# Message passing over 212,500 edges on one core: the main loop's transposes written as ordinary matmuls with the identity

## What is computed

```python
h = relu(layernorm(x))
def layer(h, row, col, dist, ...):
    edge_in = concatenate([h[row], h[col], dist], axis=1)      # 129 columns
    e = silu(edge_in @ eW1 + eb1)                              # 128 hidden
    e = silu(e @ eW2 + eb2)
    agg = segment_sum(e, row, num_segments=12500)
    node_in = concatenate([h, agg], axis=1)
    return silu(node_in @ nW1 + nb1) @ nW2 + nb2
out = x + layer(h, src, dst, edge_weight1, ...)
```

## Time and profile before

| | |
|---|---|
| median of 3 runs | 3044.79 us |
| the three runs | 3040.09, 3044.79, 11595.62 us |
| profiled execution, span from the first to the last instruction | 3042.3 us |
| PE busy | 2652.8 us (87%), 21703 matmuls |
| PEld busy | 2068.1 us (68%), 21704 weight loads |
| DVE busy | 2125.5 us (70%) |
| ACT busy | 1601.7 us (53%) |
| POOL busy | 2012.3 us (66%) |
| mean granted TensorE clock | 0.986 of full speed |

### The profile page before, as it was taken

The page is one execution under the profiler, slowest core; times in us unless marked ns, Lnnn a source line. Parts: engine busy times, 40 slices in busy tenths (PEclk is TensorE's granted clock), DMA queues, the critical chain, the costliest instruction groups (busy, mean ns, idle before and its releaser), DMA issues.

```text
span 3042.3 us, 77490 instructions
## 1 busy us (share of the span) xinstructions
PE 2652.8 (87%) x21703; PEld 2068.1 (68%) x21704; DVE 2125.5 (70%) x7337; ACT 1601.7 (53%) x3366; POOL 2012.3 (66%) x2075
## 2 busy tenths in 40 slices
PE   7899999999688888888888888888888888888899
PEld 4555555555477777777777777777777777777776
DVE  8999999997566666666666666666666666666665
ACT  3677777777344444444444444444444444444455
POOL 1254444445677777777777777777777777777772
PEclk7999999999799999999999999999999999999999
DMA  3011111111222222222222222222222222222343
GB/s 94 20 40 27 39 28 39 34 34 30 48 59 59 60 57 59 59 60 59 58 59 59 60 60 58 58 60 59 59 59 59 59 59 58 58 59 55 77 120 103
DMA packets 366054, 171.78 MB, mean 56 GB/s; under 512 B 289494, under 2 KB 330126, under 8 KB 365934
## 3 DMA queue, kind: packets, MB, share of 16 engines
q0 software_dynamic: 69600, 123.49, 15.4%
q1 hardware_dynamic: 274142, 36.29, 7.8%
q10 hardware_dynamic: 22192, 10.53, 1.2%
HBM read 139.11 MB, written 31.04 MB: 56 GB/s over the span
## 4 chain that ended last, share of the span: by engine, by line
PE 81%; issue 11%; ACT 4%; DVE 3%; DMA 1%; POOL 0%; ACTq 0%; SPq 0%; DVEq 0%; POOLq 0%
PE bk L1208 16%; PE bk L1228 15%; PE bk L1219 13%; PE bk L1206 9%; PE bk L1196 5%; PE bk L1071 4%; PE bk L1217 3%; PE bk L1105 3%; PE bk L1137 2%; PE bk L1059 2%; PE bk L1060 2%; PE bk L1239 1%; ACT BIG L1354 1%; PE bk L1099 1%; PE bk L1274 1%
## 5 line engine op out<-in xcount | busy, mean ns | idle before, releaser
L554 POOL DMA_INDIRECT GA<-q_d,IX x1758 | 1671.5, 951 | 545.4 <-issue 533.3
L920 DVE SCALAR_TENSOR_TENSOR GA<-c_bc,EW,GA 128x128 f32<-128x128 f32 x1758 | 558.5, 349 | 432.7 <-DMA GA<-q_d,IX 429.2
L929 DVE TENSOR_TENSOR BIG<-bk,BIG 128x128 f32 x1758 | 511.4, 291 | 345.1 <-issue 156.4
L1206 PE MATMUL bk<-identf,GA 128*128 128x128 f32 x1758 | 501.2, 285 | 253.8 <-issue 240.3
L1208 PE MATMUL bk<-OHS,P 128*128 128x128 bf16 x5274 | 695.8, 225 | 0.1
L1443 ACT ACTIVATE ED<-bk,eb1c 128x512 f32<-128x512 f32 x440 | 302.1, 687 | 703.0 <-PE bk L1208 698.7
L1208 PEld LDWEIGHTS bk<-OHS,P 128*128 x5274 | 501.3, 96 | 111.3 <-issue 0.2
L1228 PE MATMUL bk<-ED 128*128 128x128 f32 x3516 | 504.7, 287 | 0.0
L519 POOL DMA_INDIRECT rec_d<-BIG,GA x208 | 246.8, 1187 | 376.9 <-issue 285.6
L1219 PEld LDWEIGHTS bk<-W,ED 128*128 128x128 f32 x3516 | 464.8, 193 | 24.3 <-issue 7.6
L1206 PEld LDWEIGHTS bk<-identf,GA 128*128 128x128 f32 x1758 | 247.5, 141 | 321.7 <-issue 297.2
(11 more groups left out here) (247 smaller groups left out, 2761.9 us busy)
## 6 DMA issues: line engine op xcount, KB each, us to landing
GA<-q_d,IX POOLq DMA_INDIRECT x1758, 2.5
q_d<-QS SPq DMA_DIRECT2D x14, 448.0 KB, 3.1
u_d<-QS ACTq DMA_DIRECT2D x98, 64.0 KB
OHS<-u_d SPq DMA_DIRECT2D x18, 256.0 KB, 3.1
rec_d<-ED SPq DMA_DIRECT2D x16, 220.0 KB, 9.6
RW<-rec_d SPq DMA_DIRECT2D x110, 32.0 KB
rec_d<-BIG,GA POOLq DMA_INDIRECT x208, 2.4
HT<-hT_d ACTq DMA_DIRECT2D x99, 32.0 KB
```

The costliest lines, as they stand in the source:

```text
L554: e.indirect_dma_start(G[k % 4 * U + u], None, q_d, bass.IndirectOffsetOnAxis(ap=IX[g // BG % 2][:, k * U + u:k * U + u + 1], axis=0))\
L920: ins = e.scalar_tensor_tensor(out=G[k % 4 * U + u], in0=c_bc[:, :], scalar=ew[:, w:w + 1], in1=G[k % 4 * U + u], op0=ALU.mult, op1=ALU.add)
L929: e.tensor_tensor(AGG[:, ds(v, P)], banks[6 + k % 2][:, u * P:(u + 1) * P], AGG[:, ds(v, P)], ALU.add).then_inc(s["ad"], 1)
L1206: e.matmul(z, G[k * U + u], identf[:, :], is_transpose=True, start=True, stop=False)
```

## The change

The diff is complete. `TPb` becomes the whole of bank 0 as fp32, so that the turned one-hots stand there as fp32 values; `tcopy` is not touched and reads them as fp32. In `mA` the four bf16 transposes become ordinary bf16 matmuls with the identity, and in `mB` the fp32 transpose that opens each tile's sum becomes an ordinary fp32 matmul with the identity. The waits, the order and all other work stay.

```diff
@@ -263,7 +263,7 @@
-        TPb = banks[0][:, :].bitcast(bf16)[:, 0:512]
+        TPb = banks[0]
@@ -1193,7 +1193,7 @@
                 for u in range(tiles(g)):
-                    last = e.transpose(TPb[:, u * P:(u + 1) * P], OHb[k][:, u, :], identb[:, :])
+                    last = e.matmul(TPb[:, u * P:(u + 1) * P], OHb[k][:, u, :], identb[:, :], start=True, stop=True)
                 last.then_inc(s["tp"], 1)
@@ -1203,7 +1203,7 @@
                     z = banks[2][:, u * P:(u + 1) * P]
-                    e.matmul(z, G[k * U + u], identf[:, :], is_transpose=True, start=True, stop=False)
+                    e.matmul(z, G[k * U + u], identf[:, :], start=True, stop=False)
                     for q in range(3):
                         last = e.matmul(z, P3[q][:, ds(v, HF)], OHT[k % 2][:, u * P:(u + 1) * P],
                                         start=False, stop=(q == 2))
```

## The result

The changed kernel takes 3051.69 us (median of 8 runs, 3050.11 to 3053.89); the kernel before, run beside it, 3040.68 us (median of its 8; one of them, 11595.62 us, is far off and left out of the ratio; without it the median is 3040.12). The ratio is 1.0037, 95% interval [1.0028, 1.0046]: 11.0 us slower, or 0.37%, and within 2%. The interval reaches from 8.5 to 14.0 us. The forecast was +10.6 us. The 3055 us that were predicted start from 3044.79 us, a median of three runs, and lie 3.3 us too high; that starting point alone is 4 us too high. The profiled execution has a span of 3050.3 us and took 3052.16 us.

The account below looks back on a forecast made before the run. POOL's gathers were taken to bound the loop and PE the end: zero in the loop and for the one-hots, 9.8 plus 0.8 us at the end, together +10.6 us, predicted 3055 us, range 3046 to 3080.

Parts of the forecast that it names:

- What bounds the loop: In the main loop POOL's gathers, four of 1.25 us, set a group's time of 5.0 us, although PE looks busier.
- I am wrong if POOL waits for PE in the loop: Sign against the forecast in the main loop, where POOL was expected to have almost no wait for PE.
- Two instructions for one: In `mB` each fp32 transpose becomes an ordinary matmul of two instructions, so line 1206 shows 3516 instead of 1758.
- The price of a tile: Each `mB` tile gains 0.12 us of PE work (0.11 to 0.13), 0.48 us a group; wider bounds 0.06 to 0.24.
- The threshold for 2%: In the loop, roughly 0.18 us extra a tile would make the kernel slower by over 2% (61 us).
- The loop's slack: PE needs 19.75 us for four loop groups, POOL gives 20.1: 0.3 us to spare, no time added, idle 0.57 to 0.1.
- the two rivals that break it: In the loop PE overtakes POOL, about 3230 us, chance 0.09; or lands just over its pace, near 3075, chance 0.07.
- The end: In the last, unrolled groups PE sets the time: 20.5 groups add 9.8 us, three groups before them 0.8 us.
- The one-hots at zero: In `mA` ordinary bf16 matmuls cost the same as bf16 transposes, and ACT's copy from the fp32 bank adds zero.
- The rule of a fourfold transpose: Rival: `mB`'s ordinary fp32 matmul costs four times the transpose, 0.44 us against 0.11, giving 3389 us; chance 0.02.

Follow-up runs that it names:

- e3b: The changed kernel with the gathered rows of the last 24 groups back on fp32 transposes: 3040.92 us, ratio 0.9998 to the kernel before.
- e9: The changed kernel with one more ordinary fp32 matmul of the same rows ahead of each loop tile's own, result overwritten: 3081.87 us, ratio 1.0134 to the kernel before.
- the first comparison: Follow-up runs on a chip of their own, against the kernel before, with the changes tried by halves and by loop or end; the kernel before took 3562 us there.
- e6: The changed kernel with a group's four ordinary fp32 matmuls issued first and its twelve bf16 matmuls behind them: 3048.03 us, ratio 1.0023 to the kernel before.
- e4b: The changed kernel with fp32 transposes of gathered rows in the loop, ordinary fp32 matmuls in the last 24 groups alone: 3052.97 us, ratio 1.0038 to the kernel before.
- the second comparison: Follow-up runs on another chip, e3b, e4b and e6 among them, against the kernel before, which took 3041 us there.
- e7: The kernel before with a group's four fp32 transposes issued ahead of its twelve bf16 matmuls: 3039.86 us, ratio 0.9999 to the kernel before.
- e1: The changed kernel with fp32 transposes kept for the gathered rows, only the one-hots' transposes made ordinary matmuls: 3562.99 us, ratio 1.000 to the kernel before.

## Why the prediction was right, and where its steps were off

**What bounds the loop: right.** POOL's waits named it against the busy shares, e3b shows that the loop's ordinary matmuls are free, and e9 that the next step past the limit is paid. "I am wrong if POOL waits for PE in the loop" did come true on the chip of the first comparison, where the kernel before waits too.

**Two instructions for one: right,** 3516 of them.

**The price of a tile: right in kind, mis-sized.** The term was 0.12 us (0.11 to 0.13), from fp32 matmuls that stand in a row. Where it is paid, a tile went from 0.285 to 0.445 us, 0.16 more, but the group's first tile only 0.11: 0.58 us a group in place of 0.48. e6 brings a pair down to 0.22 us by its place alone. The rows to take stood in the earlier trace rows: eight L1219 take 0.89 us, and eight L1228, which follow the short bf16 matmuls of L1196, 0.95. I spread the 0.06 over all eight as 0.119 each. In that trace the first L1228 has the next start behind it after 0.165 us and each of the others after 0.112, in all 16 groups from 2905 to 3000 us: 0.05 us are due once, wherever an fp32 matmul follows short bf16 ones, and that is three times a group here. By these numbers a pair behind short bf16 matmuls costs 0.222 + 0.055 us, the transpose 0.11, and a group gains 3 x 0.165 + 0.11, 0.6 us. The threshold for 2%, 0.18 us a tile, in the rivals, was also a slip: by the same formula it is 0.17.

**The loop's slack: the conclusion holds, the reading failed.** I had 0.3 us to spare in four groups and PE's wait going from 0.57 to 0.1 us. It went to 0.51. I had read one tile of the loop, 0.44 us; it was the first of its group, and the next ones took mostly 0.37, as from 1308.72 on:

```profile
1309.09 0.28 PE L1206 MATMUL bk<-identf,GA 128*128 128x128 f32 x1
...
1309.46 0.28 PE L1206 MATMUL bk<-identf,GA 128*128 128x128 f32 x1
```

The trace has three register instructions of PE's sequencer in each tile there, 0.12 us apart, and a bf16 matmul starts behind each of them. Now a tile takes 0.47 us and then 0.445, and the register instructions pass beside the longer matmuls. So `mB` grew by about 0.03 + 3 x 0.075 = 0.25 us a group in the loop, not by the 0.48 of the sum or the 0.58 of the end. Part of that came back as shorter gaps behind it: PE's idle time ahead of L1196 from 1100 to 2840 us fell from 31.7 us to this:

```profile
PE bk L1196 <- issue: 3.5, 21, 0.2
```

By e9 four groups need 16.8 us with the change made, not 19.75, so the cover that I called thin was some 3 us. The chance of 0.16 for the two rivals that break it rested on the thin cover and looks high by this. It isn't a bound for every chip: in the first comparison POOL waited for PE, and the loop paid 17 us.

**The end: right in total, by luck in part.** Expected were 9.8 + 0.8 us. With the measured price the same sum gives 20.5 x 0.58 = 11.9 us and 3 x 0.58 - 0.6 = 1.1, so 13.0; measured were 11.0, and 12.1 in e4b. The price was 2.4 us too low, and against it stands that the first unrolled groups still had idle time to lose in the changed kernel: PE waits 0.34 us at 2891.16 and 0.51 us at 2901.62, and is saturated only from there. The interval of 8.5 to 14.0 us can't tell 10.6 from 13.0; the rows of the groups can.

```profile
2891.16 0.46 PE L1206 MATMUL bk<-identf,GA 128*128 128x128 f32 x2 [0.34 <-issue]
...
2901.62 0.46 PE L1206 MATMUL bk<-identf,GA 128*128 128x128 f32 x2 [0.51 <-issue]
```

The spans of the two profiled executions differ by only 8.0 us, since 3042.3 us is long for the kernel before: in the second comparison its spans lie around 3039. By group 400 its gathers in that trace stood 3.7 us behind those of the changed kernel; e7, with transposes throughout, stood 3.4 us ahead of it as well. So this is scatter.

**The one-hots at zero: right** (e1, e3b). **The rule of a fourfold transpose: fell.** In fp32 the transpose costs 0.11 us here and the ordinary pair 0.22 to 0.27, a factor of 2 to 2.4. The Trainium skill's "TensorE: Matmul & The Clock Gate", Terms, calls transpose mode four times faster for fp32: these rows agree with the direction and not with the factor.

## What to carry to other kernels

Ask for each stage which engine cannot wait, by its own waits and not by its busy share: the same edit was free in 416 groups paced by a gather and paid in the last 24, where PE sets the pace. PE's time in a stretch where something else paces it is no measure of what it needs; load it until it saturates, as e9 does, before calling a cover thin. An fp32 transpose of 128 columns is cheaper as a transpose (0.11 us here) than as an ordinary matmul (0.22 to 0.27), and where PE is the bound, ordinary fp32 matmuls stand best behind one another. When two groups of equal instructions in a trace differ by a little, look at the single starts before spreading the difference: here it sat in the first of eight.

## What was not expected of the hardware

- An ordinary fp32 pair costs 0.22 us behind fp32 matmuls or behind a transpose, and 0.27 us behind short bf16 matmuls, since its first weight load starts only 0.06 us ahead of it there; a transpose costs 0.11 to 0.12 us in each place that is shown.
- The same program took 3041 us beside the changed kernel and in two comparisons, and 3562 us in another, on another chip, with narrow scatter there (3559.16 to 3565.25 us in 21 runs). There the semaphores of `mA`, `mB` and `mD` came up to some 3 us late and together. As one comparison ran on that chip, the record doesn't tell whether the chip or its state then did it; but a cover seen on one chip isn't proof for another.
